# A graph network's VectorE work beside the gathers in smaller pieces, biases tile by tile, node rows loaded behind the edges

## The chip, the cores and the metric

The kernel runs on one core of a Trainium2 chip. The core has five engines with a queue of instructions each: PE (TensorE, matrix products into PSUM), DVE (VectorE), ACT (ScalarE), POOL (GpSimd) and SP (SyncE, which here only issues DMAs and waits). The engines meet through semaphores. The metric is the device time of one execution in microseconds (us); lower is better.

## The reference

3125 nodes with 256 features pass through two layers of a graph network, with 50000 edges sorted by target. What is computed:

```python
edge_index = jnp.stack([src, dst])
xn = _layernorm(x, axis=-1)
x = x + _L0_gnn_ref(xn, ...) + _L0_mix_ref(xn[None], ...)[0]
x = x + _L0_ffn_ref(_layernorm(x, axis=-1)[None], ...)[0]
xn = _layernorm(x, axis=-1)
x = x + _L1_gnn_ref(xn, edge_index, edge_attr_2, ...) + _L1_mix_ref(xn[None], ...)[0]
x = x + _L1_ffn_ref(_layernorm(x, axis=-1)[None], ...)[0]
```

The change touches three parts of it. In `_L0_mix_ref` (linear attention, 4 heads of 32) the queries go through a softmax over their 32 features and are scaled:

```python
q = jax.nn.softmax(q, axis=-2) * SCALE
k = jax.nn.softmax(k, axis=-1)
context = jnp.einsum('bhdn,bhen->bhde', k, v)
out = jnp.einsum('bhde,bhdn->bhen', context, q)
```

In `_L1_ffn_ref` a small graph attention over 32768 random edges gives the router's scores, and four experts give the output, each with an output bias `b2[ei]`:

```python
e = jax.nn.leaky_relu(a_src[src] + a_dst[dst], negative_slope=0.2)
e_max = jax.ops.segment_max(e, dst, num_segments=M)
ee = jnp.exp(e - e_max[dst])
denom = jax.ops.segment_sum(ee, dst, num_segments=M)
...
hh = jax.nn.gelu(x @ W1[ei] + b1[ei], approximate=False)
out = out + g[..., None] * (hh @ W2[ei] + b2[ei])
```

The edges of that router come unsorted, so the kernel sorts them by target itself.

## The kernel before, in words

The nodes lie in 25 tiles of 128 rows (`T` = 25, `P` = 128), in `c.X` with 25 x 256 values in each partition. The order of each engine's work is written out by hand; there is no scheduler. The program is a row of blocks, and between two blocks all engines meet at a barrier. Within a block POOL runs a queue of its own of indirect DMAs (one of 128 rows each, with a one-element memset `breathe` behind it) while the other engines go through several stages.

- `stage_setup` (block 0): SP loads the node rows `c.X` (L135, and L139 for the last 53 rows) and waits for them (L140, seen as L129 at the end of the block); POOL makes the constants (L149 to L166).
- Block 1 (L894): `rank_stage` ranks the edges by tile on the DVE (`Ranking.load` issues its DMAs: keys, values, payload, and at L240 the store of empty slots); `norm_stage` is the first layer norm; `mix0_stage` is the linear attention, with the query softmax at L1062 to L1068 (reduce maximum, subtract it with the two-input operation L1063, ACT's exponential, reduce sum, multiply at L1068); `sort_stage` sorts the router's edges: `hot_tile` (in the trace key_tile_hot, 256 x 25 values in a partition, L616) marks the tile of each key, and `prefix` (L601) runs a scan over 1625 values four times. Beside all this `scatter_records` (L786) puts 391 times 128 edge records into DRAM, from the moment the first 64 columns are ranked (`e.head`); every fourth waits for the landing of those eight before.
- Block 2: the first graph sum, 416 gathers (L1144). Block 3: the first layer's experts, with 391 further scatters. Block 4: the second graph sum, 440 gathers (L2016). The change leaves these three alone.
- Block 5 (L2977): `attend_stage`. POOL scatters the 25 segment starts (L2451), gathers 256 columns of source rows (L2463) in 11 chunks (`SLOT_CUTS`), and, after the running sums of all chunks are stored, 25 columns of node states (L2474). The gathers of chunk k wait until chunk k-2 has been taken (`taken`). PE and ACT do the four experts in 20 turns of 5 tiles (`turns_of_experts`), expert x in turns 5x to 5x+4; ACT copies a tile's output from PSUM into `experts_out` or, for the last expert, into `xT`, and counts it in `y_done`. ACT does the exponential of chunk k behind turn `EXP_BEHIND[k]`: the order on ACT is fixed, so a chunk whose arguments are late holds up ACT's next turn. The DVE goes through `chunk(k)`: arguments (L2651 to L2671), then the multiplication with the exponentials (L2677), then twenty scans (L2685). Behind the chunks 2, 5 and 8 (`BIAS_BEHIND`) it adds the bias of one whole expert in one operation of 25 x 256 values (L2696), and in the tail, beside the gathers of the node states, that of the last expert in two of 25 x 128 (L2735). `from_row_hot` (L2605) is the identity matrix times a row number, 25 x 128 values, which PE reads behind turn 0.
- Then the gates (`gates1_stage`) and the gated sum with the stores (`finish_stage`).

```python
EXP_BEHIND = (3, 5, 7, 8, 10, 12, 14, 15, 17, 19, 19)
BIAS_BEHIND = {2: 0, 5: 1, 8: 2}
CHUNK_TILES = 5
```

## Time and profile before

| what | value |
|---|---|
| median of 3 runs | 3193.21 us (3189.69 to 3198.11) |
| the profiled execution | 3194.32 us, its span in the profile 3192.6 us |
| busy | PE 68%, PE weight load 50%, DVE 54%, ACT 33%, POOL 73% of the span |
| mean granted clock of PE | 0.816 |
| POOL's scatters and gathers | L786 x782, L2016 x440, L1144 x416, L2463 x256, mean 964 to 1058 ns |

How to read it: the profile is of one execution. A row of the timeline has the start (us from the span's start), the duration, the engine (SPq is SP's queue, PEld the weight load), the line of the code, the operation, what it writes <- what it reads, the shapes and, in brackets, how long the engine was idle before it and for whom. Operations of one kind that follow each other are merged (x4). The duration of a POOL row is the time in which the engine prepares the DMA; the landing comes later. No engine is busy all the time, since the blocks have different limits.

### The profile page before, as it was taken

To read this page: it belongs to the slowest core of one execution; us is meant where nothing else is said; L and a number is where in the kernel's file an instruction comes from. 1 tells how busy PE (TensorE), PEld (TensorE's weight loads), DVE (VectorE), ACT (ScalarE), POOL (GpSimd) and SP (SyncE) were. 2 spreads that over 40 slices of the span, in tenths; PEclk is the share of its full clock that TensorE was granted. 3 is DMA by queue.
4 is the path that set the end of the run, shared out by engine and by line. 5 is a ranking of instruction groups with operands and counts; after the bars stand their busy time and mean duration, and the time that the engine had idled before them with its cause. 6 is when DMAs were issued, how large, how long until landed. Compare 5 with 4: busy or idle time off the path is not lost. (4 is left out here: it accounts for less than half of the span.)

```text
span 3192.6 us, 35999 instructions
## 1 busy us (share of the span) xinstructions
PE 2176.8 (68%) x9610; PEld 1611.4 (50%) x9611; DVE 1712.2 (54%) x4546; ACT 1053.7 (33%) x2867; POOL 2317.1 (73%) x4104
## 2 busy tenths in 40 slices
PE   0283461177777756989999984976667655999930
PEld 0162351044344425878888863554444444777720
DVE  7746897166678873101111043668888883232337
ACT  0121352065555521122222212216566541343310
...
GB/s 59 18 42 2 6 3 2 173 91 105 105 104 103 103 80 32 52 175 205 192 192 198 154 83 79 57 44 51 50 50 51 52 22 38 19 33 29 20 13 41
DMA packets 173603, 233.48 MB, mean 73 GB/s; under 512 B 59898, under 2 KB 136828, under 8 KB 172412
## 3 DMA queue, kind: packets, MB, share of 16 engines
...
q1 hardware_dynamic: 98332, 119.57, 11.9%
...
q14 instruction: 108, 0.88, 0.1%
...
## 5 line engine op out<-in xcount | busy, mean ns | idle before, releaser
L786 POOL DMA_INDIRECT slots_gnn<-rec_gnn,slot_row_gnn x782 | 785.2, 1004 | 239.0 <-issue 148.6
L2016 POOL DMA_INDIRECT arena<-table,slot_gnn x440 | 465.5, 1058 | 162.1 <-issue 84.1
L1144 POOL DMA_INDIRECT rows_gnn<-support,slot_gnn x416 | 400.9, 964 | 106.4 <-issue 58.4
L1189 PE MATMUL banks<-rows_gnn,one_hot 128*128 128x256 f32 x832 | 312.0, 486 | 222.0 <-DMA rows_gnn<-support,slot_gnn 217.4
L1189 PEld LDWEIGHTS banks<-rows_gnn,one_hot 128*128 128x128 f32 x832 | 159.6, 228 | 352.6 <-DMA rows_gnn<-support,slot_gnn 214.4
L2103 PE MATMUL banks<-weighted,one_hot 128*128 128x260 f32 x880 | 284.1, 481 | 56.5 <-ACT weighted L2078 55.5
L2463 POOL DMA_INDIRECT source_rows<-table_g,source_router x256 | 262.7, 1026 | 51.4 <-issue 42.1
L764 POOL MEMSET idle<- 128x1 bf16 x2044 | 254.7, 125 | 0.8
L2103 PEld LDWEIGHTS banks<-weighted,one_hot 128*128 128x128 f32 x880 | 195.5, 234 | 114.9 <-issue 81.8
L1590 ACT ACTIVATE hidden_private<-banks,b_private 128x256 f32<-128x256 f32 x256 | 121.2, 473 | 362.7 <-PE banks L1558 362.7
L1558 PE MATMUL banks<-slot_xT,w_private 128*128 128x256 f32 x1024 | 229.2, 383 | 1.0 <-DVE slot_xT L1603 1.0
L1568 PE MATMUL banks<-w_private,hidden_private 128*128 128x256 f32 x1024 | 226.3, 379 | 0.0
L1558 PEld LDWEIGHTS banks<-slot_xT,w_private 128*128 128x128 f32 x1024 | 196.9, 192 | 28.2 <-issue 1.4
L1568 PEld LDWEIGHTS banks<-w_private,hidden_private 128*128 128x128 f32 x1024 | 192.5, 190 | 24.5
L742 ACT ACTIVATE lane_one_hot<-lanes_apart,packed_router,packed_minus_router 128x128 bf16<-128x128 bf16 x512 | 203.9, 480 | 2.1
L1221 DVE TENSOR_TENSOR x<-banks,x 128x256 f32 x416 | 175.8, 423 | 51.2 <-PE banks L1189 5.3
L736 ACT ACTIVATE lanes_apart<-iota,slot_lane_router 128x128 bf16<-128x128 bf16 x256 | 81.5, 389 | 361.3 <-PE banks L752 219.3
L2557 PE MATMUL banks<-xT,w 128*128 128x320 f32 x640 | 182.2, 441 | 15.2 <-DMA w<-in_w2e 11.5
L2568 PE MATMUL banks<-w,hidden 128*128 128x256 f32 x800 | 175.9, 379 | 0.0
L2078 ACT ACTIVATE weighted<-arena,edge_weight 128x65 f32<-128x65 f32 x660 | 166.3, 335 | 6.5 <-PE banks L2103 5.6
L1209 DVE TENSOR_SCALAR one_hot<-iota,slot_gnn 128x128 f32<-128x128 f32 x416 | 119.6, 361 | 84.2 <-PE banks L1189 80.8
L2568 PEld LDWEIGHTS banks<-w,hidden 128*128 128x128 f32 x800 | 152.3, 190 | 22.5
...
## 6 DMA issues: line engine op xcount, KB each, us to landing
...
slots_gnn<-rec_gnn,slot_row_gnn POOLq DMA_INDIRECT x782
...
arena<-table,slot_gnn POOLq DMA_INDIRECT x440
rows_gnn<-support,slot_gnn POOLq DMA_INDIRECT x416, 2.8
```

The costliest lines, as they stand in the source:

```text
L742: op = act.activation(self.lane_hot[:, b % 2, k, q, :], self.apart[:, b % 2, k, :], ACT.Relu, bias=e.value[:, q, j:j + 1], scale=e.minus[: ...
L764: pool.memset(c.idle[:, c.breaths:c.breaths + 1], 0.0)
L786: pool.indirect_dma_start(e.slots, bass.IndirectOffsetOnAxis(e.rows[:, j:j + 1], 0), e.rec[:, j, :], None)\
L1144: pool.indirect_dma_start(e.rows_in[:, k, :], None, table, bass.IndirectOffsetOnAxis(row, 0))\
L1189: mm = pe.matmul(bank_of(k // per), hot[:, k, :], e.rows_in[:, k, :], start=k % per == 0, stop=k % per == per - 1)
L1558: mm = pe.matmul(c.bank[:, f % 4, 0:GROUP], w1[:, b, k, f * P:(f + 1) * P], xT[:, b, k, :], start=k == 0, stop=k == KD - 1)
L1568: mm = pe.matmul(c.bank[:, 6 + j, 0:D], hid[:, f, j * P:(j + 1) * P], w2[:, b, f, :], start=f == 0, stop=f == FC - 1)
L2016: pool.indirect_dma_start(c.raw[:, t % RAW_RING, :], None, c.table1, bass.IndirectOffsetOnAxis(row, 0))\
L2103: mm = pe.matmul(c.bank[:, k // per, 0:AGG], hot[:, k, :], val[:, k, :, :].rearrange("p h f -> p (h f)"), start=k % per == 0, stop=k % per ...
L2463: pool.indirect_dma_start(rows[:, k % 2, j - lo, :], None, c.table_g, bass.IndirectOffsetOnAxis(er.idx[:, j:j + 1], 0)).then_inc(rows_in[h ...
L2557: mm = pe.matmul(c.bank[:, 2 * (f % 2) + half, 0:HALF_CHUNK], w1[:, x % 2, k, f * P:(f + 1) * P], c.xT[:, k, at + half * HALF_CHUNK:at + ( ...
L2568: mm = pe.matmul(c.bank[:, 4 + row % 2, 0:D], hid[:, f, :, :].rearrange("p a n -> p (a n)")[:, t * P:(t + 1) * P], w2[:, x % 2, f, :], sta ...
```

## The change

Five edits, none of which changes what is computed:

1. The node rows are no longer loaded in `stage_setup`; `Ranking.load` issues them in block 1 behind the keys, values and payload, ahead of the store of the empty slots, and the first `norm_stage` waits for them (`rows_loaded`).
2. In `mix0_stage` the subtraction and the multiplication of the queries are done in 13 pieces of two tiles (256 values; the last 128). In `sort_stage` `hot_tile` is made in 16 pieces of 400 values, and each of the four prefix scans in 9 pieces of 3 tiles (195 values; the last 65), which is possible because `gate` is zero at the start of each tile.
3. `from_row_hot` is made by 25 operations of 128 values with one tensor input and a scalar for each partition.
4. The expert output biases are added tile by tile (256 values), behind the scans of chunk k for all tiles of the turns up to `EXP_BEHIND[k]`: 20 behind chunk 0, then 10, 10, 5, 10, 10, 10, 5, 10, 10 and none behind chunk 10.
5. With that the last expert's bias no longer stands in the tail.

In each run of pieces only the last one signals; the pieces do not wait for one another. Before each bias addition stands a wait on `y_done`.

```diff
@@ -123,25 +123,16 @@
     c.head64 = c.sb(ctx, "head64", [P, P])
     c.idle = c.sb(ctx, "idle", [P, BREATHS], BF16)
     c.breaths = 0
-    load_sem = c.sem(ctx, "setup_loaded")
+    c.rows_loaded = c.sem(ctx, "node_rows_loaded")
     const_sem = c.sem(ctx, "constants_made")
-    zero_sem = c.sem(ctx, "tail_zeroed")
+    c.tail_zeroed = c.sem(ctx, "tail_zeroed")
     with ExitStack() as s, nc.Block() as block:
         c.iota_i = c.sb(s, "iota_i", [P, 512], I32)
         c.part_i = c.sb(s, "part_i", [P, 1], I32)
 
-        @block.sync
-        def _(sp):
-            sp.dma_start(c.X[:, 0:T - 1, :], c.a["x"][0:(T - 1) * P, :].rearrange("(t p) d -> p t d", p=P))\
-              .then_inc(load_sem, 16)
-
-            sp.wait_ge(zero_sem, 1)
-            sp.dma_start(c.X[0:LAST, T - 1, :], c.a["x"][(T - 1) * P:N, :]).then_inc(load_sem, 16)
-            sp.wait_ge(load_sem, 32)
-
         @block.vector
         def _(dve):
-            dve.memset(c.X[:, T - 1, :], 0.0).then_inc(zero_sem, 1)
+            dve.memset(c.X[:, T - 1, :], 0.0).then_inc(c.tail_zeroed, 1)
 
         @block.gpsimd
         def _(pool):
@@ -230,11 +221,16 @@
         self.past_ready = c.sem(ctx, f"past_ready_{e.name}")
         self.past_summed = c.sem(ctx, f"past_summed_{e.name}")
 
-    def load(self, sp):
-        e = self.e
+    def load(self, sp, rows=False):
+        c, e = self.c, self.e
         sp.dma_start(self.key[:], e.key).then_inc(self.key_in, 16)
         sp.dma_start(self.val[:], e.val).then_inc(self.loaded, 16)
         sp.dma_start(self.pay[:], e.payload).then_inc(self.loaded, 16)
+        if rows:
+            sp.dma_start(c.X[:, 0:T - 1, :], c.a["x"][0:(T - 1) * P, :].rearrange("(t p) d -> p t d", p=P))\
+              .then_inc(c.rows_loaded, 16)
+            sp.wait_ge(c.tail_zeroed, 1)
+            sp.dma_start(c.X[0:LAST, T - 1, :], c.a["x"][(T - 1) * P:N, :]).then_inc(c.rows_loaded, 16)
         sp.wait_ge(self.empty, 1)
 
         sp.dma_start(e.slots[0:P * e.tiles, :].rearrange("(p t) w -> p (t w)", p=P),
@@ -370,7 +366,7 @@
 
     @block.sync
     def _(sp):
-        r.load(sp)
+        r.load(sp, True)
         meet(sp, met, met_n)
 
     @block.scalar
@@ -597,8 +593,12 @@
                 ch.then(dve.tensor_copy(seen[:, s, :, 0], seen[:, s - 1, :, STRIPE]))
             else:
                 ch.then(dve.memset(seen[:, 0, :, 0], 0.0))
-            run = seen[:, s, :, :].rearrange("p t j -> p (t j)")
-            ch.then(dve.tensor_tensor_scan(run, gate[:].rearrange("p t j -> p (t j)"), run, 0.0, ALU.mult, ALU.add))
+            for lo in range(0, T, SCAN_PIECE):
+                hi = min(lo + SCAN_PIECE, T)
+                run = seen[:, s, lo:hi, :].rearrange("p t j -> p (t j)")
+                op = dve.tensor_tensor_scan(run, gate[:, lo:hi, :].rearrange("p t j -> p (t j)"), run, 0.0,
+                                            ALU.mult, ALU.add)
+            ch.then(op)
 
         ch.then(dve.tensor_copy(ident16[:], c.ident[:]))
         dve.wait_ge(loaded, 32)
@@ -613,9 +613,13 @@
             ch.then(dve.tensor_scalar(signs[:, :, w], low_i[:], 2.0, -1.0, ALU.mult, ALU.add))
         ch.then(dve.tensor_scalar(low_i[:], key[:], 7, None, ALU.logical_shift_right))
         ch.then(dve.tensor_copy(tile[:], low_i[:]))
-        ch.then(dve.tensor_tensor(hot_tile[:], c.iota[:, 0:T].rearrange("p (o t) -> p o t", o=1).to_broadcast([P, J, T]),
-                                  tile[:].rearrange("p (j o) -> p j o", o=1).to_broadcast([P, J, T]), ALU.is_equal))
-        dve.sem_inc(consts, 1)
+        some = [P, TILE_PIECE, T]
+        for lo in range(0, J, TILE_PIECE):
+            op = dve.tensor_tensor(hot_tile[:, lo:lo + TILE_PIECE, :],
+                                   c.iota[:, 0:T].rearrange("p (o t) -> p o t", o=1).to_broadcast(some),
+                                   tile[:, lo:lo + TILE_PIECE].rearrange("p (j o) -> p j o", o=1).to_broadcast(some),
+                                   ALU.is_equal)
+        op.then_inc(consts, 1)
         ch.then(dve.memset(gate[:], 1.0))
         ch.then(dve.memset(gate[:, :, 0:1], 0.0))
         for b in range(2, batches + 2):
@@ -693,6 +697,8 @@
 BATCH = 4
 STRIPE = 64
 KEY_BITS = 12
+TILE_PIECE = 16
+SCAN_PIECE = 3
 START_W = 5
 STATE_W = 24
 
@@ -821,6 +827,8 @@
     @block.vector
     def _(dve):
         ch = Chain(dve, step)
+        if first:
+            dve.wait_ge(c.rows_loaded, 32)
         for t in range(T):
             dve.bn_stats(stats[:, t, :], X[:, t, :]).then_inc(step, 1)
         ch.n += T
@@ -1057,15 +1065,20 @@
         dve.tensor_tensor(k, k, c.bank[:, 5:6, 0:HID0].to_broadcast([P, TM, HID0]), ALU.subtract)\
             .then_inc(k_shift, 1)
         qh = q[:, 0:T, :].rearrange("p t (h d) -> p t h d", h=HEADS0)
-        qs = [P, T, HEADS0, DH0]
-        by_head = lambda b: b[:].rearrange("p (t h o) -> p t h o", h=HEADS0, o=1).to_broadcast(qs)
+        spans = [(lo, min(lo + 2, T)) for lo in range(0, T, 2)]
+        by_head = lambda b, lo, hi: b[:, lo * HEADS0:hi * HEADS0].rearrange("p (t h o) -> p t h o", h=HEADS0, o=1)\
+            .to_broadcast([P, hi - lo, HEADS0, DH0])
         ch.then(dve.tensor_reduce(q_max[:].rearrange("p (t h) -> p t h", h=HEADS0), qh, AX.X, ALU.max))
-        dve.tensor_tensor(qh, qh, by_head(q_max), ALU.subtract).then_inc(q_shift, 1)
+        for lo, hi in spans:
+            op = dve.tensor_tensor(qh[:, lo:hi], qh[:, lo:hi], by_head(q_max, lo, hi), ALU.subtract)
+        op.then_inc(q_shift, 1)
         dve.wait_ge(q_exp, 1)
         ch.then(dve.tensor_reduce(q_sum[:].rearrange("p (t h) -> p t h", h=HEADS0), qh, AX.X, ALU.add))
         ch.then(dve.reciprocal(q_sum[:], q_sum[:]))
         ch.then(dve.tensor_scalar(q_sum[:], q_sum[:], DH0 ** -0.5, None, ALU.mult))
-        dve.tensor_tensor(qh, qh, by_head(q_sum), ALU.mult).then_inc(q_ready, 1)
+        for lo, hi in spans:
+            op = dve.tensor_tensor(qh[:, lo:hi], qh[:, lo:hi], by_head(q_sum, lo, hi), ALU.mult)
+        op.then_inc(q_ready, 1)
         dve.wait_ge(ctx_ready, 1)
         ch.then(dve.reciprocal(inv_k[:], c.bank[:, 7, 0:1]))
         dve.tensor_tensor(ctx_t[:], c.bank[:, 6, 0:HID0], c.head32[:], ALU.mult).then_inc(ctx_out, 1)
@@ -2347,7 +2360,6 @@
 SLOT_CUTS = (0, 24, 48, 72, 96, 120, 144, 168, 192, 216, 240, 256)
 EXP_BEHIND = (3, 5, 7, 8, 10, 12, 14, 15, 17, 19, 19)
 LOAD_BEHIND = {2: 2, 5: 3}
-BIAS_BEHIND = {2: 0, 5: 1, 8: 2}
 EXPERTS1, FF1 = 4, 512
 EARLY_TURN, EARLY_CARRY = 0, 2
 PARTS = 3
@@ -2601,10 +2613,9 @@
         ch.then(dve.tensor_copy(begun[:, :, 0:NE1], far))
         dve.sem_inc(starts_ready, 1)
         ch.then(dve.memset(ones16[:], 1.0))
-        shape = [P, T, P]
-        dve.tensor_tensor(from_hot[:], c.ident[:].rearrange("p (o n) -> p o n", o=1).to_broadcast(shape),
-                          er.from_row[:].rearrange("p (t o) -> p t o", o=1).to_broadcast(shape), ALU.mult)\
-           .then_inc(diag_ready, 1)
+        for t in range(T):
+            op = dve.tensor_scalar(from_hot[:, t, :], c.ident[:], er.from_row[:, t:t + 1], None, ALU.mult)
+        op.then_inc(diag_ready, 1)
         ch.then(dve.memset(peak[:, 0, :, 0:1], 0.0))
         ch.then(dve.memset(carry_t[:], 0.0))
         for b, (lo, hi) in enumerate(pieces):
@@ -2687,13 +2698,17 @@
                                                 ALU.mult, ALU.add)
             op.then_inc(state_ready, 1)
 
+        biased = 0
         for k, (lo, hi) in enumerate(cuts):
             chunk(k, lo, hi)
-            if k in BIAS_BEHIND:
-                x = BIAS_BEHIND[k]
+            if k == 0:
                 dve.wait_ge(b2_in, 16)
-                dve.wait_ge(y_done, (x + 1) * T)
-                ch.then(dve.tensor_tensor(y[:, x, :, :], y[:, x, :, :], b2[:, x:x + 1, :].to_broadcast([P, T, D]), ALU.add))
+            for at in range(biased, (EXP_BEHIND[k] + 1) * CHUNK_TILES):
+                x, t = at // T, at % T
+                dve.wait_ge(y_done, at + 1)
+                dve.tensor_tensor(kept(x, t), kept(x, t), b2[:, x, :].rearrange("p (k d) -> p k d", k=KD), ALU.add)
+                biased = at + 1
+        assert biased == EXPERTS1 * T
 
         dve.wait_ge(state_ready, len(cuts))
         last = len(cuts) - 1
@@ -2728,11 +2743,6 @@
             if q < PARTS - 1:
                 ch.then(dve.tensor_tensor(carry[:], carry[:], carry16[:, q, :], ALU.subtract))
         dve.sem_inc(table_ready, 1)
-        last_x = EXPERTS1 - 1
-        dve.wait_ge(y_done, EXPERTS1 * T)
-        for k in range(KD):
-            half = c.xT[:, k, :].rearrange("p (t d) -> p t d", d=P)
-            ch.then(dve.tensor_tensor(half, half, b2[:, last_x:EXPERTS1, k * P:(k + 1) * P].to_broadcast([P, T, P]), ALU.add))
         dve.wait_ge(looked, 1)
         for b, (lo, hi) in enumerate(((0, FIRST), (FIRST, T))):
             op = dve.tensor_copy(carried[:, lo:hi, :].rearrange("p t w -> p (t w)"), c.bank[:, b, 0:(hi - lo) * STATE_W])
```

SP at the start of the program. In before the node rows come first and a barrier stands behind them; `key_gnn`, `val_gnn` and `pay_gnn` are the edges, `slots_gnn` the store of the empty slots:

```order
L135 DMA x<-in_x 128x24x256
L139 DMA x<-in_x 53x256 [waits tail_zeroed]
L129 UNCONDITIONAL_BRANCH [waits setup_loaded]
L371 UNCONDITIONAL_BRANCH [waits barrier_Pool_Activation_PE_DVE_SP_release]
L235 DMA key_gnn<-in_src 128x391
L236 DMA val_gnn<-in_dst 128x391
L237 DMA pay_gnn<-in_edge_weight 128x391
L240 DMA slots_gnn<-fill_gnn 128x1664 [waits empty_slots_gnn0]
```

The same place after the change:

```order
L367 UNCONDITIONAL_BRANCH [waits barrier_Pool_Activation_PE_DVE_SP_release]
L226 DMA key_gnn<-in_src 128x391
L227 DMA val_gnn<-in_dst 128x391
L228 DMA pay_gnn<-in_edge_weight 128x391
L230 DMA x<-in_x 128x24x256
L233 DMA x<-in_x 53x256 [waits tail_zeroed]
L236 DMA slots_gnn<-fill_gnn 128x1664 [waits empty_slots_gnn0]
```

The loads of x now stand behind the three of the edges, and the wait for them is no longer SP's.

DVE in `sort_stage`, at the first of the four prefix scans (`xT` is the room in which they run), before:

```order
L590 SCALAR_TENSOR_TENSOR equal_earlier<-banks,before 128x512
L599 MEMSET xT 128x25
L601 SCALAR_TENSOR_TENSOR xT<-same_tile,xT 128x1625
L582 TENSOR_TENSOR key_lane_hot<-iota,sort_lane 128x512
L590 SCALAR_TENSOR_TENSOR equal_earlier<-banks,before 128x512
```

and after:

```order
L586 SCALAR_TENSOR_TENSOR equal_earlier<-banks,before 128x512
L595 MEMSET xT 128x25
L599 SCALAR_TENSOR_TENSOR xT<-same_tile,xT 128x195 x8
L599 SCALAR_TENSOR_TENSOR xT<-same_tile,xT 128x65
L578 TENSOR_TENSOR key_lane_hot<-iota,sort_lane 128x512
L586 SCALAR_TENSOR_TENSOR equal_earlier<-banks,before 128x512
```

The one scan of 1625 values became eight of 195 and one of 65 at the same place.

DVE in `attend_stage`, at the end of chunk 9 and the beginning of chunk 10, before:

```order
L2685 SCALAR_TENSOR_TENSOR running_sums<-edge_weights,running_sums,weighted_rows 128x24 x4
L2685 SCALAR_TENSOR_TENSOR running_sums<-edge_weights,running_sums 128x24
L2651 TENSOR_TENSOR edge_weights<-source_rows,target_score 128x4x16
L2652 TENSOR_SCALAR source_lifted<-source_rows,lift 128x4x16
L2655 COPY running_peak<-running_peak 128x4
L2659 SCALAR_TENSOR_TENSOR running_max<-same_segment,running_max,source_lifted 128x16 x4
L2662 SCALAR_TENSOR_TENSOR running_peak<-running_max,lift,target_score 128x4x16
```

and after (`b_1` is the bias, `xT` here the last expert's output):

```order
L2696 SCALAR_TENSOR_TENSOR running_sums<-edge_weights,running_sums,weighted_rows 128x24 x4
L2696 SCALAR_TENSOR_TENSOR running_sums<-edge_weights,running_sums 128x24
L2709 TENSOR_TENSOR xT<-xT,b_1 128x2x128 x10
L2662 TENSOR_TENSOR edge_weights<-source_rows,target_score 128x4x16
L2663 TENSOR_SCALAR source_lifted<-source_rows,lift 128x4x16
L2666 COPY running_peak<-running_peak 128x4
L2670 SCALAR_TENSOR_TENSOR running_max<-same_segment,running_max,source_lifted 128x16 x4
```

Ten additions now stand between the scans of chunk 9 and the first operation of chunk 10.

## Rows read from the trace of the kernel before

**Rows 1.** Timeline, stage 1 ends: start, us, engine, line, operation, tiles, count.

```profile
543.25 0.29 DVE L687 TENSOR_SCALAR slot_column_router<-sort_low_i 128x256 f32<-128x256 int32 x1
...
591.07 0.96 POOL L786 DMA_INDIRECT slots_gnn<-rec_gnn,slot_row_gnn  x1 [0.19 <-issue]
```

**Rows 2.** Waits of SP, 0 to 100 us: waited for, us, times, longest.

```profile
SPq L129 <- DMA x<-in_x: 7.3, 1, 7.3
```

**Rows 3.** Timeline of the start: last constant on POOL, first scatter.

```profile
5.41 0.29 POOL L166 TENSOR_SCALAR_AFFINE_SELECT head<-head 128x128 f32<-128x128 f32 x1
...
58.23 1.18 POOL L786 DMA_INDIRECT slots_gnn<-rec_gnn,slot_row_gnn  x1 [52.52 <-DVEq L347]
```

**Rows 4.** Timeline of stage 1: long DVE operations and the scatters beside them.

```profile
227.44 3.49 DVE L1063 TENSOR_TENSOR qkv<-qkv,q_max 128x3200 f32<-128x3200 f32 x1
227.63 4.13 POOL L786 DMA_INDIRECT slots_gnn<-rec_gnn,slot_row_gnn  x1 [0.19 <-issue]
239.64 3.13 POOL L786 DMA_INDIRECT slots_gnn<-rec_gnn,slot_row_gnn  x1 [0.19 <-DMA slots_gnn<-rec_gnn,slot_row_gnn]
...
350.19 6.54 POOL L786 DMA_INDIRECT slots_gnn<-rec_gnn,slot_row_gnn  x1 [0.19 <-issue]
...
382.26 3.17 POOL L786 DMA_INDIRECT slots_gnn<-rec_gnn,slot_row_gnn  x1 [0.19 <-issue]
...
460.49 3.55 POOL L786 DMA_INDIRECT slots_gnn<-rec_gnn,slot_row_gnn  x1 [0.19 <-issue]
```

**Rows 5.** Timeline: short two-input DVE operations and the gathers beside them.

```profile
63.80 1.16 POOL L786 DMA_INDIRECT slots_gnn<-rec_gnn,slot_row_gnn  x1 [0.19 <-issue]
64.12 0.88 DVE L319 TENSOR_TENSOR seen_gnn<-seen_gnn,in_tile_gnn 128x327 f32<-128x327 f32 x2
...
2849.00 0.79 DVE L2685 TENSOR_TENSOR_SCAN running_sums<-edge_weights,running_sums,weighted_rows 128x24 f32<-128x24 f32 x4
2849.38 0.94 POOL L2463 DMA_INDIRECT source_rows<-table_g,source_router  x1 [0.19 <-issue]
```

**Rows 6.** Groups of POOL, 58 to 115 us: count, busy us, mean ns.

```profile
L786 POOL DMA_INDIRECT slots_gnn<-rec_gnn,slot_row_gnn x43 | 44.7, 1040 | 59.7 <-DVEq L347 52.5 <-issue 5.3
```

**Rows 7.** Groups of DVE over the whole span.

```profile
L1088 DVE TENSOR_TENSOR y<-y,rows 128x256 f32 x25 | 10.6, 425 | 0.9
L2696 DVE TENSOR_TENSOR experts_out<-experts_out,b 128x6400 f32<-128x6400 f32 x3 | 20.4, 6794 | 0.0
```

**Rows 8.** Timeline of the last stage: gathers beside the long operations.

```profile
2694.93 3.88 POOL L2451 DMA_INDIRECT starts_router<-segment_starts,start_at_router  x1 [104.64 <-DVEq L2602]
...
2851.89 7.18 POOL L2463 DMA_INDIRECT source_rows<-table_g,source_router  x1 [0.19 <-DMA source_rows<-table_g,source_router]
```

**Rows 9.** Timeline of the last stage: exponentials, and PE behind a late one.

```profile
2984.62 4.47 PE L2557 MATMUL banks<-xT,w 128*128 128x320 f32 x16
2989.58 0.36 ACT L2524 ACTIVATE edge_weights<-edge_weights 128x192 f32<-128x192 f32 x1 [3.09 <-DVE edge_weights L2671]
2992.10 0.83 PEld L2557 LDWEIGHTS banks<-xT,w 128*128 128x128 f32 x4 [3.52 <-ACT hidden L2514]
...
3056.37 0.34 DVE L2651 TENSOR_TENSOR edge_weights<-source_rows,target_score 128x96 f32<-128x96 f32 x1 [19.05 <-DMA source_rows<-table_g,source_router]
3061.20 0.90 DVE L2677 TENSOR_TENSOR weighted_rows<-source_rows,edge_weights 128x384 f32<-128x384 f32 x1 [1.63 <-ACT edge_weights L2524]
3065.25 0.24 DVE L2685 TENSOR_TENSOR_SCAN running_sums<-edge_weights,running_sums 128x24 f32<-128x24 f32 x1
...
3074.64 0.28 DVE L2651 TENSOR_TENSOR edge_weights<-source_rows,target_score 128x64 f32<-128x64 f32 x1 [9.15 <-DMA source_rows<-table_g,source_router]
3081.18 0.23 DVE L2685 TENSOR_TENSOR_SCAN running_sums<-edge_weights,running_sums 128x16 f32<-128x16 f32 x1
```

**Rows 10.** Timeline behind the last chunk: the gathers of the node states.

```profile
3089.14 3.48 POOL L2474 DMA_INDIRECT marks_then_nodes<-states_router,end_at_router  x1 [0.19 <-issue]
3092.92 3.22 POOL L2474 DMA_INDIRECT marks_then_nodes<-states_router,end_at_router  x1 [0.19 <-issue]
```

## The prediction

> **What bounds the kernel now.** I read the page's waits by engine first, then the timeline at the places where one stage hands over to the next, and last the durations of single gathers beside what the DVE does. The program is a chain of five blocks with barriers between, and an edit pays only where its engine ends the block. Block 1 (ranking, norm, mix0, sort, with 391 record scatters on POOL beside them) ends with POOL: the last sort step of the DVE is over at 543.5, the last scatter at 592.0 [rows 1]. So block 1 has 48.5 us of room on the DVE and none on POOL. It starts late for another reason: SP sits 7.3 us on the landing of the node rows [rows 2] before the barrier, although POOL's last constant is made at 5.7, and the first scatter starts at 58.2, released by the DVE's ranking [rows 3].
>
> Beside it stands what a gather costs. An ordinary scatter takes 0.96 us [rows 1]. Seven in block 1 take 3.1 to 6.5 us, each with one long DVE operation of two SBUF inputs over it: it starts 0.19 us behind the subtraction at 227.44 (3.49 us) and ends at 231.76, 0.83 us after it [rows 4]. I read that as a lock: the scatter waits until the running operation is over, and then does nearly its whole work. In the last block the same is seen three times beside the bias additions (7.18 us for a gather, additions of 6.79 us) [rows 7, 8], once beside from_row_hot (3.88 us) [rows 8], and twice in the tail (3.48 and 3.22 us) [rows 10].
>
> What makes pieces promising is [rows 5]: at 2849.38 a gather takes 0.94 us in the middle of twenty scans of two inputs each that follow one another without a wait; at 63.80 a scatter takes 1.16 us though a second pair of operations begins at 64.12, before it ended. It waited for the operation in flight, not for the run.
>
> **Part 1, node rows behind the edges: -7.3 us.** The setup block then ends with POOL's constants, and ranking, and with it the first scatter, moves forward by SP's wait of 7.3 us. The 3 MB now stand on SP's queue behind key, value and payload and ahead of the store of the empty slots. That store must have landed before the first scatter. The 3 MB were in 13.1 us after the start when they were first on the queue (5.8 + 7.3); some 7 us later they and the store are still far ahead of the scatter at 50.9. The norm stage reads the rows after 100 us. No cost.
>
> **Part 2, pieces in block 1: -16.2 us.** Seven scatters took 4.13, 3.13, 6.54 and, for the four scans, 3.17, 3.21, 3.22 and 3.55 us [rows 4] (there the first and the last of the four), 26.95 us in all; seven ordinary ones are 6.7, so 20.2 us are stall. The DVE pays for pieces: 256 elements take 0.43 us [rows 7], two of 327 take 0.88 together [rows 5]. The two query operations become 13 each (5.3 us at most, from 3.5), key_tile_hot 16 of 400 elements (8.6 us by the 0.44 of 327), each scan 9 pieces, which I put at 0.55 us, 5 us (an estimate between those rows). That is 39 us of DVE work, some 14 us more than before, against 48.5 us of room [rows 1], of which 23.5 us go with POOL's gain: hidden. Beside those 39 us run 31 scatters. In 58 to 115 us, where the DVE does short operations without rest, a scatter takes 1.040 us on average [rows 6], 0.08 more than alone. Bounds: nothing, and half of a 0.6 us piece (0.3). I take 0.13, near the row and above it since there one-input operations lie between: 4.0 us. Gain 20.2 - 4.0 = 16.2, between 10.9 and 20.2.
>
> The Trainium skill, "SBUF — State Buffer", section on SBUF's two separate sides, says the same of the port pair that DVE and GpSimd share: an exclusive lock for a whole instruction, against a DVE operation with two SBUF inputs. Rows 4 and 5 agree, and by it only the instruction counts, not the run.
>
> **Part 3, from_row_hot and the three bias additions: -9.6 us of 21.5.** On POOL the stalls are 3.88 - 0.96 = 2.9 and three times 7.18 - 0.94 = 6.2, 18.7; 21.6 us. But POOL's last row gather isn't what ends this block any more. Chunk k's exponential stands on ACT behind expert turn 3, 5, 7 ... 19, and the turns run at PE's pace. Chunk 9 began at 3056.37 and still waited for ACT until 3061.20 [rows 9]. With gathers 20 us earlier its rows lie ready for 20 us and the exponential behind turn 19 decides. One turn gets faster: behind turn 15 ACT stood 3.09 us for a late chunk, PE idled 3.0 us and then took 6.27 us for 16 matmuls that take 4.47 otherwise [rows 9]. With chunk 7 in time, both go: r = 4.8 us, and chunk 9 multiplies at 3056.4. Its scans end 4.3 us later (3061.20 to 3065.49), 3060.7. Then come ten bias additions of turns 18 and 19, between chunk 9 and chunk 10 on the DVE and now on the path: 10 x 0.43 = 4.3 us [rows 7], 3065.0. Chunk 10 needs 6.8 us (3074.64 to 3081.41) [rows 9]: 3071.8 against 3081.4. Gain = 9.1 + r - b, b being the ten additions. With r = 3.0 and b = 6.0 (0.60 an addition, if each wait on y_done costs) 6.1; with r = 4.8 and b = 3.5, 10.4. The waits on y_done are all met: each run stands behind the exponential of its chunk, which ACT does after the copies. The 90 other additions (39 us) lie in DVE time in which it waits for rows or for ACT; if the run of 20 (8.6 us) behind chunk 0 makes chunk 1 start late, chunk 1's exponential still stands two turns further on. The 25 one-input pieces of from_row_hot are needed by PE only behind turn 0: hidden.
>
> The Trainium skill, "VectorE: DVE Perf Modes", section on the TRN2 errata, speaks against this edit: an SBUF operation pays a fixed 58 cycles at 0.96 GHz each time, and tiles should have 512 elements or more. By its formula the ten additions are 10 x 314 / 0.96 = 3.3 us and the total gain would be 1.0 us larger; no rule of cost there undoes the stalls.
>
> **Part 4, the last bias additions leave the tail: -4.8 us.** The two gathers took 3.48 + 3.22 us [rows 10], against 1.9. POOL is what the DVE then waits for, so all of it is on the path.
>
> **Sum.** 7.3 + 16.2 + 9.6 + 4.8 = 37.9 us. The profiled execution took 3194.32 us (span 3192.6), which gives 3156.4; the median of the runs is 1.1 us lower, so 3155.3. By the bounds 29.1 to 42.7, 3150.5 to 3164.1.
>
> **Rivals.**
> A, the expert turns don't hold the last block: if turns or exponentials come early enough that POOL's 21.5 us arrive whole, 11.9 us more, 3143.4. For it: other turns could lose small stalls too. Against it: chunk 9 waited for ACT already before [rows 9].
> B, slower: the port isn't given back between two operations issued without a wait. Then a run stalls a gather for all its length: in block 1 5.3, 5.3, 8.6 and 4 x 5 us against 3.5, 3.5, 6.8 (6400 elements, as in rows 7) and 4 x 3.5, +11.4 instead of -16.2, with -7.3 for the load +4.1; in the last block 100 x 0.43 = 43 us of additions against 20.4 [rows 7], +22.6, less 2.9 and 4.8. Together +19: 3212. It decides as soon as a 0.43 us run keeps a gather out longer than one operation. Rows 5 speak against it, though with scans of 0.2 us in the clearest case.
> C, every scatter or gather beside a piece waits half of it and more (0.3 us and over) and the ten additions cost 6 us: parts 2 and 3 give 10.9 and 6.1, 3164 and up to 3170 with the spread of runs.
> D, no change: what POOL gains comes back as another wait, PE's granted clock in the unchanged blocks above all. The mean time would stay near 3190. Nothing in the trace names such a wait.
>
> **How the numbers follow.** Forecast 0.66, A 0.08, B 0.04, C 0.18, D 0.04. The range takes the bounds (3150.5 to 3164.1) and the spread of the three runs (3189.7 to 3198.1, -3.5 and +4.9): 3146 to 3170; it leaves out A, B, D. About 0.3% (9.6 us) is what a measurement of this kernel can tell from no change: faster 0.92, within 0.04, slower 0.04.
>
> **What would show it.** Right: the first scatter near 51; no scatter over 1.7 us beside the query, key_tile_hot and same_tile pieces; POOL's last scatter 23 us earlier, near 569, the DVE's sort within a few us of 543; in the last block PE without the idle 3 us behind turn 15, row gathers done about 20 us earlier against the block's start, and the DVE going from the exponential of chunk 9 through ten additions to chunk 10 without a gap; node-state gathers all at 0.95. Wrong: gathers beside the pieces that last as long as the run (B); a DVE that waits for rows at chunk 9 or 10 (A); a wait of the scatters on the slot store, or of the DVE on the keys, at 20 to 50 us (part 1).

## The result, and the profile after

The changed kernel takes 3173.4 us (median of 5 runs, 3166.0 to 3179.5) against 3194.8 us of the kernel before (5 runs): ratio 0.9933, 95% interval 0.9912 to 0.9955. That is 21.4 us faster where 37.9 were forecast, and outside the range of 3146 to 3170. The profiled execution took 3173.4 us, span 3171.6, so the two profiles can be compared stage by stage.

Block 1 did what was forecast. Timeline of POOL and the DVE in the changed kernel (start, us, engine, line, operation, count): the first scatter, the query subtraction and its scatters, key_tile_hot and its scatters, the last scatter.

```profile
50.86 1.18 POOL L792 DMA_INDIRECT slots_gnn<-rec_gnn,slot_row_gnn  x1 [45.15 <-DVEq L343]
...
220.03 3.78 DVE L1073 TENSOR_TENSOR qkv<-qkv,q_max 128x256 f32<-128x256 f32 x11
220.22 1.06 POOL L792 DMA_INDIRECT slots_gnn<-rec_gnn,slot_row_gnn  x1 [0.19 <-issue]
221.59 1.03 POOL L792 DMA_INDIRECT slots_gnn<-rec_gnn,slot_row_gnn  x1 [0.19 <-issue]
...
342.37 7.86 DVE L618 TENSOR_TENSOR key_tile_hot<-iota,sort_tile 128x400 bf16<-128x400 f32 x16
344.86 1.34 POOL L792 DMA_INDIRECT slots_gnn<-rec_gnn,slot_row_gnn  x1 [1.56 <-issue]
346.50 1.16 POOL L792 DMA_INDIRECT slots_gnn<-rec_gnn,slot_row_gnn  x1 [0.19 <-issue]
...
565.72 0.95 POOL L792 DMA_INDIRECT slots_gnn<-rec_gnn,slot_row_gnn  x1 [0.19 <-issue]
```

The first scatter starts 7.4 us earlier than in [rows 3], the last one ends at 566.7 instead of 592.0 [rows 1]: 25.3 us, so 18 us are the pieces. Where [rows 4] had 4.13, 3.13, 6.54 and 3.17 us there are 1.03 to 1.34. Blocks 2 to 4 carry this on: block 5 begins on POOL at 2670.9, 24.0 us before the 2694.93 of [rows 8].

Block 5 then lost instead of winning. From POOL's first indirect DMA in it to the end of its last gather it takes 428.2 us; before it took 424.9, and the forecast was 410.5 (424.9 - 9.6 - 4.8; the expectations below say 410.6). Groups of the changed kernel (count, busy us, mean ns, idle before), then the timeline at two of the ten runs of bias additions (L2709), and below it the long addition of the kernel before, beside which stood the gather of 7.18 us at 2851.89 [rows 8]:

```profile
L2475 POOL DMA_INDIRECT source_rows<-table_g,source_router x256 | 273.1, 1067 | 51.6 <-issue 42.9
...
L2709 DVE TENSOR_TENSOR experts_out<-experts_out,b 128x256 f32<-128x256 f32 x75 | 25.6, 415 | 0.0
```

```profile
2756.38 6.78 DVE L2709 TENSOR_TENSOR experts_out<-experts_out,b 128x256 f32<-128x256 f32 x20
2756.67 7.29 POOL L2475 DMA_INDIRECT source_rows<-table_g,source_router  x1 [0.19 <-issue]
...
2950.06 3.41 DVE L2709 TENSOR_TENSOR experts_out<-experts_out,b 128x256 f32<-128x256 f32 x10
2950.34 3.95 POOL L2475 DMA_INDIRECT source_rows<-table_g,source_router  x1 [0.19 <-issue]
```

```profile
2851.45 6.80 DVE L2696 TENSOR_TENSOR experts_out<-experts_out,b 128x6400 f32<-128x6400 f32 x1
```

A gather that starts beside twenty additions ends 0.8 us after the last of them, just as it did beside the one operation of 6.8 us. Nine of the ten runs do this (7.29; 3.48, 3.67 and four times 3.95 or 3.96; twice 2.28 beside runs of five), 26.4 us of stall against the 18.7 of the three long ones. What that costs is seen at chunk 7 and at chunk 10:

```profile
2961.17 4.47 PE L2569 MATMUL banks<-xT,w 128*128 128x320 f32 x16
...
2975.11 0.36 ACT L2536 ACTIVATE edge_weights<-edge_weights 128x192 f32<-128x192 f32 x1 [12.06 <-DVE edge_weights L2682]
2977.63 6.95 PE L2569 MATMUL banks<-xT,w 128*128 128x320 f32 x16 [11.99 <-ACT hidden L2526]
...
3047.40 0.90 DVE L2688 TENSOR_TENSOR weighted_rows<-source_rows,edge_weights 128x384 f32<-128x384 f32 x1 [8.38 <-ACT edge_weights L2536]
3051.60 3.41 DVE L2709 TENSOR_TENSOR xT<-xT,b 128x256 f32<-128x256 f32 x10
3052.16 3.67 POOL L2475 DMA_INDIRECT source_rows<-table_g,source_router  x1 [0.19 <-issue]
3058.71 0.28 DVE L2662 TENSOR_TENSOR edge_weights<-source_rows,target_score 128x64 f32<-128x64 f32 x1 [3.70 <-DMA source_rows<-table_g,source_router]
```

In [rows 9] ACT stood 3.09 us for chunk 7; now it stands 12.06 us, PE with it, and PE comes back at a granted clock of 0.65 (from 2977.6 to 2984.6; it was 1.00, the full 2.4 GHz, before PE stood, and is again behind 2984.6), so that 16 matmuls take 6.95 us. The tail is as forecast: 25 node-state gathers with a mean of 943 ns, in place of the 3.48 and 3.22 us of [rows 10].

### The profile page after: what moved, and what is told of

Read it like the earlier page. It is cut to its first block and busy times, and to the rows that moved or that the text cites. A ratio compares the mean times of both kernels' runs of the same rounds, so it can differ in the third digit from the quotient of the medians.

```text
span 3171.6 us, 36182 instructions
## 1 busy us (share of the span) xinstructions
PE 2174.3 (69%) x9611; PEld 1607.3 (51%) x9611; DVE 1724.1 (54%) x4736; ACT 1053.2 (33%) x2867; POOL 2303.5 (73%) x4104
## 3 DMA queue, kind: packets, MB, share of 16 engines
q10 hardware_dynamic: 1440, 9.06, 0.7%
## 5 line engine op out<-in xcount | busy, mean ns | idle before, releaser
L792 POOL DMA_INDIRECT slots_gnn<-rec_gnn,slot_row_gnn x782 | 767.5, 981 | 232.2 <-issue 145.8
L2475 POOL DMA_INDIRECT source_rows<-table_g,source_router x256 | 273.1, 1067 | 51.6 <-issue 42.9
L2580 PEld LDWEIGHTS banks<-w,hidden 128*128 128x128 f32 x800 | 152.2, 190 | 22.6
```

The costliest lines, as they stand in the source:

```text
L792: pool.indirect_dma_start(e.slots, bass.IndirectOffsetOnAxis(e.rows[:, j:j + 1], 0), e.rec[:, j, :], None)\
L2475: pool.indirect_dma_start(rows[:, k % 2, j - lo, :], None, c.table_g, bass.IndirectOffsetOnAxis(er.idx[:, j:j + 1], 0)).then_inc(rows_in[h ...
L2580: mm = pe.matmul(c.bank[:, 4 + row % 2, 0:D], hid[:, f, :, :].rearrange("p a n -> p (a n)")[:, t * P:(t + 1) * P], w2[:, x % 2, f, :], sta ...
```

## The experiments

A word on the chips, without which the numbers can't be understood. The ratios below are each to runs of the kernel before on the same chip. On the chips of e1 to e12 the kernel before took 4582 to 4621 us; on those of the result and of e13 to e19, 3191 to 3195. How gathers and additions meet is the same on both, the totals are not:

```
kernel                     before    this      ratio, 95% interval
changed kernel             3194.8    3173.4    0.9933  0.9912 to 0.9955
e13 gap, last ten late     3192.0    3150.0    0.9871  0.9849 to 0.9893
e18 gap                    3190.8    3153.1    0.9869  0.9846 to 0.9892
e19 chained, last ten late 3190.8    3152.6    0.9871  0.9849 to 0.9894
e5  bias as before         4612.3    4621.3    1.0016  0.9999 to 1.0033
e6  chained                4612.3    4626.6    1.0035  1.0022 to 1.0049
e7  chained, last ten late 4612.3    4620.9    1.0023  1.0006 to 1.0040
e11 changed kernel again   4582.0    4575.8    0.9993  0.9979 to 1.0008
e12 chained, last ten late 4582.0    4596.3    1.0031  1.0016 to 1.0047
```

**Is it the waits on y_done, or the second operand?** e1 waits once a run, e3 adds one column of b2, broadcast (the bias is wrong: left out is each column's own value).

```diff
# e1_wait_once
+            if biased < (EXP_BEHIND[k] + 1) * CHUNK_TILES:
+                dve.wait_ge(y_done, (EXP_BEHIND[k] + 1) * CHUNK_TILES)
-                dve.wait_ge(y_done, at + 1)
# e3_broadcast
-                dve.tensor_tensor(kept(x, t), kept(x, t), b2[:, x, :].rearrange("p (k d) -> p k d", k=KD), ALU.add)
+                dve.tensor_tensor(kept(x, t), kept(x, t), b2[:, x:x + 1, 0:1].to_broadcast([P, KD, P]), ALU.add)
```

> The changed kernel with one wait on y_done ahead of each run of bias additions, in place of one ahead of each addition. In the changed kernel the gather beside the run of 20 took 7.29 us, those beside runs of 10 took 3.5 to 4.0. Theory W (the satisfied wait between two additions is what keeps the gather out, since the pieces of block 1 have none): gathers beside the runs take at most 1.3 us and the time falls to about 3158. Theory O (the second operand, a whole row of values and no broadcast, keeps the port between two operations): the gathers take 7.3 and 4.0 us as before, time 3166 to 3180.

> The changed kernel with one value of the bias, broadcast over the 256 columns, as the second operand of each bias addition: the output lacks the real bias in the experts' output, all else is kept, with the wait ahead of each addition. Theory O: a broadcast second operand gives the port back between two operations, gathers beside the runs at most 1.3 us, about 3158. Theory W: 7.3 and 4.0 us as before, 3166 to 3180.

Timeline of e1, then of e3:

```profile
4053.41 6.77 DVE L2710 TENSOR_TENSOR experts_out<-experts_out,b 128x256 f32<-128x256 f32 x20
4053.52 7.68 POOL L2475 DMA_INDIRECT source_rows<-table_g,source_router  x1 [0.19 <-issue]
```

```profile
535.60 4.31 DVE L1080 TENSOR_TENSOR qkv<-qkv,q_sum 128x256 f32<-128x256 f32 x13
537.71 3.04 POOL L792 DMA_INDIRECT slots_gnn<-rec_gnn,slot_row_gnn  x1 [1.09 <-issue]
...
4106.43 3.41 DVE L2709 TENSOR_TENSOR experts_out<-experts_out,b 128x256 f32<-128x256 f32 x10
4106.54 4.32 POOL L2475 DMA_INDIRECT source_rows<-table_g,source_router  x1 [0.19 <-issue]
```

Neither. In e1 the run of twenty and five others still keep the gather out, three let it pass (1.09 or 1.10 us). And e3 shows at 537.71 the thing in block 1 that the changed kernel escaped there: a scatter that lasts until 0.83 us behind the end of the query pieces. e4 gave the query subtraction met waits and the multiplication a plain second operand (the query's scale is left out): beside the subtraction, whose pieces still follow at 0.341 us, scatters took 0.96 to 1.09 us; beside the multiplication one took 3.00.

> The changed kernel with two edits in block 1. The 13 pieces of the query subtraction get a wait each that is already met; their second operand stays a broadcast. The 13 pieces of the query multiplication take a plain row of 256 ones as the second operand, without waits: this leaves out the division of the query softmax and its scale. Theory W: a scatter beside the subtraction run takes up to 5 us, those beside the multiplication stay at 1.03. Theory O: those beside the subtraction stay at 1.03 to 1.06, one beside the multiplication run takes 4 to 5 us. Either costs block 1 about 3 us.

**A chain of waits between the additions.**

```diff
-                dve.tensor_tensor(kept(x, t), kept(x, t), b2[:, x, :].rearrange("p (k d) -> p k d", k=KD), ALU.add)
+                ch.then(dve.tensor_tensor(kept(x, t), kept(x, t), b2[:, x, :].rearrange("p (k d) -> p k d", k=KD), ALU.add))
```

> The changed kernel with each bias addition waiting for its own end before the next is issued (a chain, as between most DVE operations here). Theory: the port is kept because the next addition overlaps the one before (they start every 0.33 us and take 0.42). With the chain they start every 0.46 us without overlap, the gathers beside the runs take at most 1.3 us, block 5 becomes about 12 to 14 us shorter than in the changed kernel, time 3158 to 3164. Rival (whatever overlap, a dense row of two-input operations keeps POOL out): 20 x 0.46 + 0.7 = 10 us for the gather beside the run of 20, block 5 some 8 us longer, 3182.

> The changed kernel with a wait for the end of the addition before ahead of every bias addition (same edit as e2_chained, now timed in rounds). Additions start every 0.457 us and no longer overlap. If the overlapping run was what kept the gathers out, all gathers beside them take 1.06 to 1.12 us, PE's turn 16 is an ordinary one again, and the time is 36 us under the kernel before, ratio 0.989 or less (the forecast of the prediction, less 1.3 us for the longer ten additions). If waits cost more than they save, as the one look of e2_chained had it (13.6 us over the kernel before), the ratio is 1.000 or more.

e2 and e6 are the same kernel. Timeline of e6 (fifteen of a run of twenty additions in its first row):

```profile
4049.39 6.84 DVE L2709 TENSOR_TENSOR experts_out<-experts_out,b 128x256 f32<-128x256 f32 x15
4049.49 1.12 POOL L2475 DMA_INDIRECT source_rows<-table_g,source_router  x1 [0.19 <-issue]
4050.91 1.07 POOL L2475 DMA_INDIRECT source_rows<-table_g,source_router  x1 [0.19 <-issue]
```

Every gather beside the runs takes 1.06 to 1.12 us: the stall is gone. Without the chain the additions start 0.333 us apart and last 0.42, so each overlaps the next; with it they start 0.457 us apart. The total did not follow (1.0035). So the chain lets the gathers in, and the total, on that chip, didn't show it. Three kernels ask why.

**What holds the time on those chips.** e5 puts the bias additions back alone, e7 is e6 with the last ten additions in the tail, e11 is the changed kernel unchanged, e12 is e7 again beside it.

```diff
# e5: the loop of before behind chunks 2, 5 and 8, and its last two in the tail
+                dve.wait_ge(y_done, (x + 1) * T)
+                ch.then(dve.tensor_tensor(y[:, x, :, :], y[:, x, :, :], b2[:, x:x + 1, :].to_broadcast([P, T, D]), ALU.add))
# e7, e12: bias(lo, hi) does the chained additions lo to hi
+        biased, held = 0, (EXP_BEHIND[-3] + 1) * CHUNK_TILES
+            upto = min((EXP_BEHIND[k] + 1) * CHUNK_TILES, held)
+            bias(biased, upto)
...
         dve.sem_inc(table_ready, 1)
+        bias(held, EXPERTS1 * T)
```

> The changed kernel with the bias additions alone put back as they were (three of 6400 elements behind chunks 2, 5 and 8, the last two in the tail); the load behind the edges and all other pieces stay. If the 20 us that are missing were lost in the bias additions (theory: a run of additions keeps the gather out as one long one does, and comes eleven times instead of five), this kernel is at or below the changed one: 24 to 27 us under the kernel before, ratio 0.992, against 0.993 of the changed one, with three gathers of 7.2 us and two of 3.3 us back and block 5 within 3 us of its length before. If the pieces of block 1 or the load cost something elsewhere, it stays above the changed kernel by the 14 us that part 3 and 4 were to bring.

> As e6_chained, and the ten additions of turns 18 and 19 stand behind the carry table in the tail, where the last bias additions stood before, instead of between chunk 9 and chunk 10. Theory: chunk 10 then waits for ACT's exponential or for nothing, and the end comes up to 4.6 us (ten at 0.457) earlier than in e6_chained; ten node-state gathers lose 0.12 us each at most, on the path. Net 3 to 4.5 us under e6_chained. Rival: ACT's exponential of chunk 10, behind turn 19, holds chunk 10 anyway; then it is within 1 us of e6_chained.

> The changed kernel itself, unchanged, beside the kernel before. Its ratio was 0.9933 where it was first measured. If this chip has the same waits as the one of the result, 0.991 to 0.996; if it is one on which ACT and PE hold blocks 1 and 5 (as the ones of e1 to e8 did), 0.999 to 1.003.

> e7_late_ten's kernel again, beside the changed one on the same chip: chained bias additions, the last ten in the tail. On a chip with the waits of the result: 15 to 20 us under the changed kernel (17.6 us that block 5 lost against the forecast, 4.6 us for the ten additions, less 1.3), ratio to before 0.987 to 0.989. On one where ACT and PE hold blocks 1 and 5: within 0.2% of the changed one.

Waits of e11, 0 to 1000 us (engine, line, waited for: us, times, longest), then the same two of the changed kernel where the result was measured:

```profile
POOL rows_gnn L1157 <- DMA slot_gnn<-slots_gnn: 303.9, 1, 303.9
ACT qkv L1026 <- remote: 231.3, 22, 19.8
```

```profile
ACT qkv L1026 <- PE banks L992: 54.8, 25, 14.0
...
POOL rows_gnn L1157 <- DMA slot_gnn<-slots_gnn: 13.3, 1, 13.3
```

There ACT stops 22 times in the query and key stage for something that the profile doesn't name ("remote"), and POOL stands 304 us behind its scatters. A shorter POOL is worth nothing: the changed kernel itself gives 0.9993. The first half of e5's expectation fails (it asked for 0.992) for this reason, and e6's with it; those of e11 and e12 had named the case. What stays open is why the chained kernels are slower there than the changed one (e12 20.6 us over e11), and what the unnamed waits are.

**Size of the pieces.** e8 does halves of 128 elements, e9 two and three tiles at once (512 and 768).

```diff
# e8_halves
+                for k2 in range(KD):
+                    dve.tensor_tensor(kept(x, t)[:, k2, :], kept(x, t)[:, k2, :], b2[:, x, k2 * P:(k2 + 1) * P], ALU.add)
# e9_two_three_tiles
+                for t, n in ((t0, 2), (t0 + 2, 3)):
+                    dve.wait_ge(y_done, x * T + t + n)
```

> The changed kernel with each bias addition cut into its two halves of 128 elements, no waits between. Theory S (a gather is let in when an operation in flight ends before the next starts; overlapping neighbours keep it out unless its start falls right): the halves overlap by a larger share and every run keeps the gather out to its end, 20 tiles some 7 to 9 us. Rival T (shorter pieces, shorter waits): gathers take under 1.3 us everywhere beside them.

> The changed kernel with each turn's five bias additions of 256 elements made two, of 512 and 768 elements, no waits between. They start some 0.6 and 0.87 us apart and still overlap by 0.08 us, a smaller share. Theory S (the overlap's share of the cadence sets how often a gather's start falls on an open boundary; 400-element pieces at 0.485 let all scatters through): most gathers take under 1.9 us. Rival (a run of additions keeps the gather out whatever the size): 7.3 us beside the run behind chunk 0 and 3.9 us beside those of two turns, as in the changed kernel.

Timeline of e8 beside its run of forty (the row counts eleven), then of e9 beside its run of eight:

```profile
4059.86 2.29 DVE L2710 TENSOR_TENSOR experts_out<-experts_out,b 128x128 f32<-128x128 f32 x11
4059.96 9.06 POOL L2475 DMA_INDIRECT source_rows<-table_g,source_router  x1 [0.19 <-issue]
```

```profile
4033.47 5.95 DVE L2711 TENSOR_TENSOR experts_out<-experts_out,b 128x512 f32<-128x512 f32 x8
4033.57 6.86 POOL L2475 DMA_INDIRECT source_rows<-table_g,source_router  x1 [0.19 <-issue]
```

Size doesn't matter in either direction; halves are worse only because the run gets longer (8.15 us). Theory S as I had written it for e9, larger pieces open more often, falls.

**An opening.** e10 puts a memset of one element behind each addition, e15 behind every third, e14 writes the additions to another target (the bias sums are left out from the twenty-first on). e13 is e10 with the last ten additions in the tail; e18 is e10's kernel, timed; e19 is e7's.

```diff
# e10, e13, e18; e15 with  if (at - biased_from) % 3 == 2:
+    gap = c.sb(ctx, "gap", [P, EXPERTS1 * T], BF16)
+                dve.memset(gap[:, at:at + 1], 0.0)
# e14_other_target
+                to = kept((at - 20) // T, (at - 20) % T) if at >= 20 else kept(x, t)
+                dve.tensor_tensor(to, kept(x, t), b2[:, x, :].rearrange("p (k d) -> p k d", k=KD), ALU.add)
```

> The changed kernel with a memset of one element a partition behind every bias addition, no waits. It has no input, so DVE holds nothing for reading there. If any operation that reads nothing between two additions is enough to let the gather in, all gathers beside the runs take 1.0 to 1.3 us as with the chain. If what keeps it out is that DVE's operations overlap at all, the runs keep it out as before (7 us and 3.9 us, plus the memsets' time).

> The changed kernel with the one-element memset behind every bias addition and the last ten additions behind the carry table in the tail. Gathers beside the additions 1.0 to 1.12 us everywhere. If the chip has the waits of the result: PE's turn 16 is an ordinary one of 17.5 us, block 5 takes 406 to 411 us instead of 428 (the forecast's 410.6, less up to 4.3 for the ten additions), ratio to before 0.987 to 0.989. If ACT and PE hold blocks 1 and 5: 1.000 to 1.004, as with the chain.

> The changed kernel with each bias addition from the twenty-first on written over an output twenty tiles earlier instead of in place, so the expert outputs are wrong (the bias sums are left out); nothing else changes. Theory I (in-place pieces keep the gather out; key_tile_hot's pieces of 400, which write elsewhere, let all scatters in): 1.0 to 1.3 us beside the runs behind chunks 1 to 10, 7.7 us only beside the run of twenty. Rival (only the start against the boundaries counts): they stay at 3.9 to 4.3 us where the gather starts 0.04 or 0.20 us ahead of a boundary.

> The changed kernel with the one-element memset behind every third bias addition only. If the memset is an opening that a waiting gather takes, a gather that starts beside a run lasts until the next memset (at most three additions, 1.0 us) and its 0.8 us: 1.1 to 2.0 us. If the memset only works by shifting the additions' starts against the gather's, some runs of ten keep it out for 3 us and more.

Timeline of e13 in the run behind chunk 0, and at turn 16; then of e14; then of e15:

```profile
2755.70 0.42 DVE L2708 TENSOR_TENSOR experts_out<-experts_out,b 128x256 f32<-128x256 f32 x1
2755.72 0.06 DVE L2709 MEMSET gap<- 128x1 bf16 x1
...
2756.21 1.06 POOL L2476 DMA_INDIRECT source_rows<-table_g,source_router  x1 [0.19 <-issue]
...
2960.65 0.36 ACT L2537 ACTIVATE edge_weights<-edge_weights 128x192 f32<-128x192 f32 x1
```

```profile
2818.94 3.40 DVE L2710 TENSOR_TENSOR experts_out<-experts_out,b 128x256 f32<-128x256 f32 x10
2819.20 3.96 POOL L2475 DMA_INDIRECT source_rows<-table_g,source_router  x1 [0.19 <-issue]
```

```profile
2789.21 1.42 DVE L2711 TENSOR_TENSOR experts_out<-experts_out,b 128x256 f32<-128x256 f32 x4
2789.47 1.62 POOL L2476 DMA_INDIRECT source_rows<-table_g,source_router  x1 [0.19 <-issue]
2790.23 0.06 DVE L2713 MEMSET gap<- 128x1 bf16 x1
2790.54 1.10 DVE L2711 TENSOR_TENSOR experts_out<-experts_out,b 128x256 f32<-128x256 f32 x3
```

The memset lasts 0.06 us and costs the DVE next to nothing (ten additions 3.51 us for 3.41), and with it all gathers beside the runs take 0.94 to 1.17 us (e10, e13, e18). In e15 the gather is kept out over three additions, and ends 0.86 us behind the start of the memset: the memset is an opening, and the gather takes it. Six of e15's ten runs show this (1.29 to 1.62 us), each ending 0.86 or 0.87 us behind the start of a memset. So it isn't the overlap by itself that keeps the gather out: with the memset the additions still start every 0.344 us and last 0.42. e14 rules out theory I: of its nine runs that write elsewhere seven keep the gather out (the run of twenty, still in place, does too).

The time comes back. Block 5, from POOL's first indirect DMA to the end of its last gather:

```
before 424.9   changed 428.2   e14 423.8   e15 409.2   e18 410.2   e13 406.8   e19 407.3   (forecast 410.5)
```

> e10_gap's kernel, timed: the changed kernel with the one-element memset behind every bias addition, the last ten still between chunk 9 and chunk 10. With e13 (3150.0, 0.9871) as the measure: block 5 takes 409 to 411 us, 2 to 4 us more than there (the ten additions, 3.5 us, on the path), so 3152 to 3154 and ratio 0.988 +- 0.002. On a chip where ACT and PE hold blocks 1 and 5: 1.000 to 1.004.

> e7's kernel on this chip: additions chained by waits, the last ten in the tail. Gathers 1.06 to 1.12 us as with the memset; the runs are a third longer (4.5 us for ten), which lies in DVE time that waits for ACT's exponential. Within 0.1% of e13: ratio 0.987 to 0.989, block 5 406 to 409 us. If waits on DVE delay chunks, 0.990 or more. On a chip where ACT and PE hold blocks 1 and 5: 1.002 to 1.004.

e18, the changed kernel with nothing but openings, has the block at 410.2 us where 410.5 were forecast, and its median, 3153.1 us, is 37.8 us under the kernel before on that chip, where 37.9 were forecast. (Its profiled execution, 3164.8 us, was the slowest of its five: blocks 2 to 4, the same code in all these kernels, took 2100.7 us in it and 2083.0 to 2090.8 us in six others on such chips. So a single total says little here, and the blocks and the medians are compared.) Its turn 16 is again one of 17.6 us, and chunk 10 follows the ten additions without a gap. e13 and e19, with those ten off the path, save 3 us more of the block in the profiles; their medians (3150.0 and 3152.6) can't tell that from e18. For the gathers, memsets and waits do the same.

**Why did block 1 escape?** e17 cuts key_tile_hot into 32 pieces of 200 elements.

```diff
-TILE_PIECE = 16
+TILE_PIECE = 8
```

> The changed kernel with key_tile_hot in 32 pieces of 200 elements instead of 16 of 400, no waits between. They start some 0.28 us apart (200/0.96 + 0.07) and take 0.36 us, so that nearly a third of each overlaps, as in the bias additions (0.333 and 0.42). If it is the short cadence that keeps scatters out, one or more of the scatters beside them lasts over 2 us where the pieces of 400 gave 1.14 to 1.34. If this kind of operation (another target of 2-byte elements, no input in full) always lets them in, all stay under 1.4 us.

Timeline of e17, then of e19, whose block 1 is the changed kernel's, pieces of 400:

```profile
340.55 8.99 DVE L618 TENSOR_TENSOR key_tile_hot<-iota,sort_tile 128x200 bf16<-128x200 f32 x32
341.66 0.95 POOL L792 DMA_INDIRECT slots_gnn<-rec_gnn,slot_row_gnn  x1 [0.19 <-issue]
342.92 1.08 POOL L792 DMA_INDIRECT slots_gnn<-rec_gnn,slot_row_gnn  x1 [0.19 <-issue]
345.56 4.82 POOL L792 DMA_INDIRECT slots_gnn<-rec_gnn,slot_row_gnn  x1 [1.44 <-issue]
```

```profile
341.51 7.86 DVE L618 TENSOR_TENSOR key_tile_hot<-iota,sort_tile 128x400 bf16<-128x400 f32 x16
342.62 1.26 POOL L792 DMA_INDIRECT slots_gnn<-rec_gnn,slot_row_gnn  x1 [0.19 <-issue]
345.26 4.93 POOL L792 DMA_INDIRECT slots_gnn<-rec_gnn,slot_row_gnn  x1 [1.26 <-issue]
```

By luck. Both rows show a scatter kept out to the end of the run, though others beside the same run got in, and the length of the pieces doesn't settle it. (e17's one run took 3189.7 us; blocks 2 to 4 had 2100.4 of them.) The query pieces, the same in all these kernels, kept a scatter out in e3, e8 and e10 (3.04, 1.87 and 2.68 us), and not in the changed kernel.

What differs is when the scatter starts against the next piece. Beside pieces of 256 elements, those that started 0.12 to 0.15 us ahead of a piece all got in after one more boundary (1.02 to 1.06 us) and then kept this distance, since a scatter and its pause are 1.34 us and four pieces too. In block 5 the start is nearly always the same, and the multiplication ahead of the scans sets it. Timeline of the changed kernel at chunk 2:

```profile
2823.10 0.90 DVE L2688 TENSOR_TENSOR weighted_rows<-source_rows,edge_weights 128x384 f32<-128x384 f32 x1 [15.34 <-ACT edge_weights L2536]
2823.37 1.39 POOL L2475 DMA_INDIRECT source_rows<-table_g,source_router  x1 [0.19 <-issue]
...
2827.29 3.40 DVE L2709 TENSOR_TENSOR experts_out<-experts_out,b 128x256 f32<-128x256 f32 x10
2827.56 3.95 POOL L2475 DMA_INDIRECT source_rows<-table_g,source_router  x1 [0.19 <-issue]
```

The multiplication holds a gather until 0.76 us behind its own end (in seven of the ten runs of this kernel), two ordinary gathers follow, and the additions begin 3.3 us behind the multiplication, so that the next gather starts 0.27 us into them. (At chunk 0 it is one gather and 2.0 us.) In e1, e3, e4 and e11 it is mostly the multiplication that releases POOL, and the gather starts 0.1 us into the additions. So gathers start 0.02 to 0.09 us or about 0.2 us ahead of an addition nearly every time, and are kept out: in 57 of 66 runs of overlapping additions over seven traces (the changed kernel, e1, e3, e4, e11, e14, e17). The start alone doesn't settle it: at 0.04 and at 0.20 us some got in, and with pieces of 400 one got in at 0.14 (e13) and the one above did not at 0.13. Nor do all operations act alike: the scans of the running sums overlap more than the additions (24 elements last 0.25 us and start every 0.156) and no gather that began among them took over 1.01 us in any trace; among the prefix scans of 195 (0.56 us, every 0.458) none took over 1.14. Why a start decides, and why scans never keep a gather out, is open.

## Why the prediction was right or wrong

**Part 1, -7.3 us**: right; 7.4 us at the first scatter, and nothing waits for the rows or the slot store.

**Part 2, -16.2 us**: right in size, 18.0 measured, inside 10.9 to 20.2. (The DVE's added work was written as some 14 us; the terms give 39.2 - 27.8 = 11.4, as in rival B, and 4.3 came. It was hidden either way.) The pieces ran faster than put down (query 4.3 us each for 5.3, key_tile_hot 7.9 for 8.6, scans 3.9 for 5), and the scatters beside them took 1.03 to 1.34 us, 0.1 us over an ordinary one, as the 0.13 had it. The reason given was wrong all the same, and the size was luck: it needed the start to fall well, which e17 and e19 show by missing it once each, at 3.9 and 4.0 us of stall.

**Part 3, -9.6 us**: the step that failed. It rests on the reading of [rows 5] that a gather waits "for the operation in flight, not for the run". The scatter at 63.80 had one more operation behind it, and the scans of 24 elements let gathers in in all traces; neither is a run of additions. On that reading chunk 7 was to be in time and r = 4.8 us to be won. In its place: seven gathers were kept out before chunk 7's last row, 22.2 us of stall against 15.3 in the kernel before (two long additions and from_row_hot); the gather of its last row ended 299.6 us into the block instead of 290.1; turn 16 took 31.9 us against 22.2 before and the 17.2 to 17.6 of an ordinary turn. So r became -9.7: 14.5 us. And the last run kept out the gather of chunk 10's rows: from the first of the ten additions to chunk 10 it took 7.1 us, not b = 4.3: 2.8 us. Together 17.3 of the 17.7 us that block 5 missed. The other terms held, as e18 shows: b was 3.5, chunk 10 begins 369.8 us into the block where the prediction had 370.1 (3065.0 - 2694.9), and from_row_hot's stall is gone in the changed kernel too (mean of its 25 gathers 968 ns). The warning that additions might make chunks late was weighed only for the DVE's time, not for POOL's.

**Part 4, -4.8 us**: right; the 25 gathers of node states took 0.943 us each for 1.136 before, 4.8 us in all.

**Rivals.** B was the mechanism, at a chance of 0.04, but in block 5 alone, and it priced a lost port at +22.6 us. It was +7.7 (26.4 against 18.7 of stall), because a run of ten takes 3.4 us and not 4.3 and one gather at most stands beside it, while the rest of the loss came through ACT's order, where an exponential that waits for rows holds the expert turns. A mixed outcome, B in one block and the forecast in the other, had no place in the range. C's 3164 to 3170 came near the time by another road: no scatter waited half a piece more. A is refuted by e13: with the rows in time the block still takes 406.8 us, held by the turns. D had no part where the result was measured, and would have been right on the chips of e5 to e12.
